# Fourteen unread bf16 products between the small matmuls of a chunked delta recurrence

## The reference

```python
def step(S, xs):
    qi, ki, ui, wi, g = xs
    attn = qi @ jnp.swapaxes(ki, -1, -2) * tril_inc
    u_t = ui - wi @ S
    o_i = qi @ S + attn @ u_t
    S_new = g[..., None, None] * S + jnp.einsum('bhck,bhcv->bhkv', ki, u_t)
    return (S_new, o_i)
S, o = jax.lax.scan(step, S0, (mv(q), mv(k), mv(u), mv(w), mv(gm)))
```

## Time and profile before

| | us |
|---|---|
| median of 3 runs | 1905.01 (1903.51 to 1905.51) |
| the profiled execution | 1906.91 |
| its span in the profile | 1905.1 |
| TensorE matmul busy in the span | 1832.0 (96%) |
| VectorE busy | 1541.2 (81%) |
| ScalarE busy | 861.9 (45%) |
| GpSimd busy | 927.4 (49%) |
| mean granted clock of TensorE | 0.973 |

### The profile page before, as it was taken

How to read it: one execution, slowest core, us unless ns; L and a number is a source line. 1 busy time by engine, 2 the same in 40 slices (tenths; PEclk the granted TensorE clock), 3 DMA queues, 4 the chain that set the end, 5 groups by cost and what they waited for, 6 DMA issues and landing times. The chain is left out here.

```text
span 1905.1 us, 45489 instructions
## 1 busy us (share of the span) xinstructions
PE 1832.0 (96%) x17954; PEld 1250.4 (66%) x17965; DVE 1541.2 (81%) x2137; ACT 861.9 (45%) x1205; POOL 927.4 (49%) x440
## 2 busy tenths in 40 slices
PE   8999999999879899999999999999999999999788
PEld 5667666666647689766666666666666676667545
DVE  4666766676777666799999999999999999999784
ACT  3666666666633345244343334443444344434401
POOL 0356655665652144045575557555755475547300
PEclk9999999999889789999999999999999999999889
DMA  3000110000030232000000000120000000000100
GB/s 141 10 15 0 52 65 14 0 14 9 7 140 3 82 116 72 12 10 15 0 14 14 14 0 14 48 70 7 7 14 14 8 6 14 14 8 2 39 13 12
DMA packets 27778, 52.64 MB, mean 28 GB/s; under 512 B 4260, under 2 KB 15285, under 8 KB 27189
## 3 DMA queue, kind: packets, MB, share of 16 engines
q1 hardware_dynamic: 27232, 51.34, 8.2%
q10 hardware_dynamic: 468, 0.16, 0.0%
HBM read 50.97 MB, written 0.52 MB: 27 GB/s over the span
## 5 line engine op out<-in xcount | busy, mean ns | idle before, releaser
L363 POOL TENSOR_TENSOR biased_sums<-biased_sums,biased_scores 128x1024 f32<-128x1024 f32 x216 | 512.7, 2374 | 138.5 <-ACT biased_scores L670 119.1
L736 DVE TENSOR_TENSOR biased_scores<-ps,bias 128x1024 f32<-128x1024 f32 x256 | 312.5, 1221 | 35.2 <-PE ps L451 33.8
L750 DVE TENSOR_TENSOR ps<-ps,biased_scores 128x512 f32<-128x512 f32 x480 | 334.7, 697 | 4.5 <-DVE ps L750 0.5
L757 DVE TENSOR_TENSOR biased_scores<-biased_scores,ps 128x1024 f32<-128x1024 f32 x256 | 306.6, 1217 | 3.5 <-PE ps L509 2.8
L670 ACT ACTIVATE biased_scores<-biased_scores 128x1024 f32<-128x1024 f32 x256 | 263.0, 1052 | 97.4 <-DVE biased_scores L757 95.3
L363 POOL TENSOR_TENSOR plain_sums<-plain_sums,plain_scores 128x1024 f32<-128x1024 f32 x104 | 246.5, 2370 | 60.6 <-ACT plain_scores L670 50.2
L750 DVE TENSOR_TENSOR ps<-ps,plain_scores 128x512 f32<-128x512 f32 x240 | 167.4, 697 | 118.1 <-ACT plain_scores L653 113.2
L451 PE MATMUL ps<-biased_queries,keys_again 64*128 64x256 f32 x2048 | 257.3, 391 | 3.9 <-DVE biased_scores L736 3.2
L463 PE MATMUL ps<-biased_scores,biased_values 128*64 128x256 f32 x2048 | 245.3, 382 | 3.6 <-ACT biased_scores L670 3.2
L398 PE MATMUL ps<-weights_again,context_again 128*64 128x128 f32 x4096 | 248.1, 274 | 0.0
L398 PEld LDWEIGHTS ps<-weights_again,context_again 128*64 128x64 f32 x4096 | 228.6, 137 | 28.7 <-issue 17.9
(11 more groups left out here) (413 smaller groups left out, 2201.4 us busy)
## 6 DMA issues: line engine op xcount, KB each, us to landing
moe_w<-in_moe_w SPq DMA_DIRECT2D x32, 256.0 KB, 2.8
weights_again<-in_wqkv SPq DMA_DIRECT2D x45, 128.0 KB, 2.2
context<-in_ctx_t SPq DMA_DIRECT2D x4, 1024.0 KB, 6.7
context_again<-in_ctx_t SPq DMA_DIRECT2D x4, 1024.0 KB, 7.5
bias<-in_fside SPq DMA_DIRECT2D x1, 4096.0 KB, 14.6
biased_w_out<-in_w_out SPq DMA_DIRECT2D x16, 256.0 KB, 2.6
context<-in_ctx_t SPq DMA_DIRECT2D x2, 1536.0 KB, 8.9
context_again<-in_ctx_t SPq DMA_DIRECT2D x2, 1536.0 KB, 9.8
```

The lines of the kernel that those rows point to most:

```text
L363: pool.tensor_tensor(both(SUM[:, :, :, :]), both((E[:, 0] if kp == 1 else SUM)[:, :, :, :]), both(E[:, kp, :, :, :]), ALU.add).then_inc(su ...
L736: dve.tensor_tensor(E[:, kp, :, :, :].rearrange("p (h t) n j -> p h t (n j)", h=2), scores_bank(kp).rearrange("p (h t n) -> p h t n", h=2, ...
L750: ins = dve.tensor_tensor(to, highest, E[:, kp, :, n, :], ALU.max)
L757: dve.tensor_tensor(at, at, c.ps[:, LOWER, :].rearrange("p (a j) -> p a j", a=HQ).unsqueeze(2) .to_broadcast([P, HQ, 2, P]), ALU.add).then ...
```

## The change

One line is added in TensorE's list of `delta_rule`: behind each `wq_step(n, b)` one product of `keep_streaming`, into bank 1. The loop has 7 values of n and 2 batches, so there are 14 of them, each a 128x128 bf16 weight load and a matmul of 512 columns. Nothing else changes: no semaphore, no buffer and no other engine's list.

```diff
                 for n in range(1, NCH):
                     for b in range(B):
                         wq_step(n, b)
+                        keep_streaming(c, pe, 1, 1)
                     if n + 1 < NCH:
                         for b in range(B):
                             ku_step(n, b)
```

## The result

| | before | after |
|---|---|---|
| median | 1903.55 us (16 runs, 1900.45 to 1908.43) | 1908.84 us (16 runs, 1905.28 to 1912.08) |
| profiled execution | 1906.91 us | 1907.35 us |
| first state product to VectorE's reader of attend | 21.95 us | 26.44 us |
| from there to the next stage's first DMA | 10.42 us | 9.71 us |

A forecast was written before the change was run, and what follows sets the result against it. It took the recurrence as a TensorE-VectorE loop with TensorE's share at half clock. Step costs 1.12 + 0.86 + 0.59 + 0 + 0.84 gave +3.4, taken as 3.2: 1905.0 + 3.2 = 1908.2 us, own range 1906.3 to 1910.5.

The forecast's parts named there:

- The clock falls at the same place and stays at half: In the recurrence: clock falls at 625.0 as before, two products in, then half speed (1.2 GHz) to the recurrence's end.
- Step 1: Recurrence's first step, full clock: VectorE's second correction covers both products; state product still read at 625.75, cost 0.
- Steps 2 and 3: Half-clock steps: TensorE alone sets 3.18 us against 2.62, two shape changes charged; +1.12 for both (0.64 to 1.60).
- Steps 4 and 5: Half-clock steps with attend's small products behind the state products: +0.86 (0.62 to 1.10) and +0.59 (0.35 to 0.83).
- Step 6: Step where VectorE's decay takes 1.22 us beside GpSimd's addition: that stall hides both products, cost 0.
- Step 7: Last states-times-rows to attend's second half: 2.06 us instead of 1.22, nothing absorbs it, +0.84 (0.60 to 1.08).
- The weight loads: Skill's rule: loads overlap matmuls only with another row group or background buffer; 128-row loads behind 64-row products not covered.
- The tail: Projections behind the recurrence: the last may meet the clock's rise up to 1.5 us better or worse.
- A: Rival: clock holds full through the recurrence, VectorE sets a 2.2 us step, -6.0 us to 1899.0; chance 0.09.
- B: Rival: clock falls, then returns midway because TensorE is hardly idle; 1900.9 us if after step 3; chance 0.06.
- C: Rival: the loop's waits, 0.54 a step at half clock, take the products whole; 0 to +1, 1905.5; chance 0.16.
- D: Rival: nothing is hidden and each change of shape empties the array; +5.5 us to 1910.5; chance 0.12.

The follow-up runs named there:

- gap-only run: Seven 512-wide products in TensorE's idle stretch ahead of the recurrence, without the change's fourteen, against the kernel before: 1902.37 us, ratio 0.9994.
- narrow kernel: The fourteen products made 128 columns wide instead of 512, against the changed kernel: 1907.71 us, ratio 1.0012 to the kernel before.
- the pairs: Both products of a step put behind batch 1's states-times-rows, against the changed kernel: 1907.89 us, ratio 1.0017 to the kernel before.
- the gap filled too: The fourteen plus seven 512-wide products in the idle stretch ahead of the recurrence, against the kernel before: 1902.36 us, ratio 0.9986.
- the tail filled too: Seven more products behind attend's second half, added to the kernel with idle stretch filled and the fourteen: 1900.87 us, ratio 0.9981 to the kernel before.
- with 56: Four 512-wide products behind each states-times-rows instead of one, against the changed kernel: 1907.39 us, ratio 1.0015 to the kernel before.

## Why the prediction was right, step by step

It said slower by 3.2 us, own range +1.3 to +5.5; the measured +5.3 (4.0 to 7.2) lies in its range, at its upper end. The mechanism was the one named. That the median itself (1908.84) came within 0.7 us of the forecast 1908.2 is luck in part: the starting point 1905.01, a median of three runs, was 1.5 us too high (16 runs gave 1903.55), and the change 2.1 us too low. By the prediction's own yardstick of 3.8 us, +5.3 is a slowdown; it gave that 0.35, and 0.52 to no change that can be told. That lean came from the same term that makes its sum too small.

- *The clock falls at the same place and stays at half.* Right, by the rows by stretch. The full clock was granted until 622.9, 2.7 us and two products into the recurrence (2.2 us before), and then not until 646.8. The gap-only run adds that filling the idle stretch would not have been enough.
- *Step 1 at no cost, where the clock is full.* Right in the number, 2.58 against 2.60, with luck in it. The sign that was named, the addition at 625.75, came 0.18 us late: the first product delayed batch 1's states-times-rows by 0.17, and changes of shape, which the step left out, cost 0.07 to 0.10 each at full clock. The wait for the second correction still covered it. And the full clock lasted 0.5 us longer than before; in the narrow kernel, where it fell 1.2 us into the recurrence, step 1 took 2.76 with smaller products.
- *Steps 2 and 3, 3.18 us each.* The mechanism right, the size not: 3.41. This is the term that was mis-sized. I charged two changes of shape a step, since I thought that small weight loads run under the wide product. None does: after each of the four sets there is 0.12. With four the prediction had written 2.94 + 0.48 = 3.42, its upper end.
- *Steps 4 and 5.* +1.02 and +0.78 against +0.86 and +0.59 predicted, and upper ends of +1.10 and +0.83; the same term.
- *Step 6 at no cost.* Right: 3.54 both times, as VectorE's 1.22 us beside GpSimd moved along.
- *Step 7.* From the first correction to the reader of attend, 3.68 against 2.57, +1.11; predicted +0.84, with an end of +1.08.
- *The sum.* 0 + 0.80 + 0.79 + 1.02 + 0.78 + 0 + 1.11 = 4.5, measured 4.49 in the recurrence, predicted 3.4 with an upper end of 4.6. The 4.6 that stood beside the sum was the better figure.
- *The weight loads.* In the Trainium skill (TensorE: Matmul & The Clock Gate, on packing small matmuls) a weight load overlaps running matmuls only where the row group differs or it goes to the background buffer. The trace agrees as far as it can tell: no load across a change between 64-row and 128-row products is covered in these rows, while in the pairs the second wide product's load is (two loads in 0.13 us at 626.25). Which buffer a load goes to, no row shows.
- *The tail.* 0.7 us shorter in the profiled execution, since the clock had come back and 2.99 us were enough for the first projections against 3.75. Such luck varies from run to run: the tails of the nine kernels lie between 8.34 and 10.94 us.
- *What remains.* The stage as a whole is 3.8 us longer in the profiled executions, and the medians differ by 5.3, with an interval from 4.0. With a tail like the one before it would be 4.5. Whether the rest is chance, an earlier fall of the clock in other executions (in pairs, with a fall 1.5 us in, step 1 took 3.35), or the clock in later stages isn't settled by these runs. The mean granted clock of all runs, 0.9762 against 0.9767, shows no loss that can be told.

Of the rivals, A (the clock holds) needs the gap filled too; with that, its 2.2 us a step was measured as 2.18 to 2.57, and its -6.0 in all as -5.3 from the first state product to the next stage, with the tail filled too. B needs more wide work than the change has. Its rule in the Trainium skill (same page, Why this matters for your kernels), to keep TensorE busy without gaps, was followed to the letter from 623 to 644.5 us, and the clock stayed at half: here the trace does not agree, and busy mostly with 64-row and 32-row products did not do. C (hidden) falls with the waits, which hold 0.54 of 1.34 us. D's 5.5 was near for the median, but for the wrong reason: 0.54 a step was hidden.

## What to carry to other kernels

Work that is meant to keep a clock up should be there before the clock falls, in the idle stretch ahead as well as in the loop. Once the clock is down, it took four times as much to bring it back. Too little is paid at half speed, less what the waits of the loop take. Price such filler by the time at the slow clock plus one change of shape on each side, and hold it against the waits of the loop. Then look who is late once the waits are used up: in two of the kernels the next state arrived late because the state products no longer had a wait between them.

## What the runs showed of the hardware

- Switching TensorE between shapes took 0.12 us at half clock, each way, between 64-row, 32-row and 128-row products alike. It showed in every step of the changed kernel. At full clock, a wide product between small ones took 0.32 us from its weight load to the next one (621.44 to 621.76 in the changed kernel), so 0.215 and 0.10.
- Small float32 products of 64 or 32 rows did not bring the clock back in 21.5 us in which TensorE was never recorded idle, even with 12 of the 14 wide products among them; with 56 it came back in the first step. They did not always prevent it: in the pairs it came back at 643.0, in the middle of attend's 32 small products, 0.9 us behind two wide ones.
- In the traces, a clock that is kept is worth 3.5 us in this recurrence (21.95 to 18.47) and about 2 in its tail (10.42 to 8.59), for 28 products that nobody reads. The median of the runs fell by 3.5 in all.
